# Down products of the first experts from parted rows and weights, as products of 512 and of 256 columns

## The reference

```python
w13_out = ragged_dot(x_sort, moe_w13, group_sizes)      # 256 -> 1024, by expert
gate, up = split(w13_out, [512])
hidden = silu(gate) * up
out_dispatch = ragged_dot(hidden, moe_w2, group_sizes)  # 512 -> 256: the down product
out = zeros.at[token_ids_sort].add(out_dispatch * w_sort)
```

## Time and profile before

| | us |
|---|---|
| median of 3 runs | 1511.56 |
| profiled execution | 1501.55 |
| its span | 1499.7 |
| TensorE busy (89%) | 1334.3 |
| VectorE busy (51%) | 766.2 |
| ScalarE busy (39%) | 585.5 |
| GpSimd busy (44%) | 654.1 |

### The profile page before, as it was taken

The page is one execution under the profiler, slowest core; times in us unless marked ns, Lnnn a source line. Parts: engine busy times, 40 slices in busy tenths (PEclk is TensorE's granted clock), DMA queues, the critical chain, the costliest instruction groups (busy, mean ns, idle before and its releaser), DMA issues. The chain is left out here.

```text
span 1499.7 us, 29032 instructions
## 1 busy us (share of the span) xinstructions
PE 1334.3 (89%) x7717; PEld 1055.5 (70%) x7718; DVE 766.2 (51%) x1962; ACT 585.5 (39%) x1311; POOL 654.1 (44%) x903
## 2 busy tenths in 40 slices
PE   7989999997979999999994998569999998577877
PEld 4656777775668888888883776258888885366655
DVE  4875888886822233223224886913333333154546
ACT  2555777775322222222222775533333332111110
POOL 1213656564023333333332763055555551655552
PEclk9998999998989999999996998579999999888989
DMA  2208222223721111111115885455555575333433
GB/s 92 63 29 326 91 88 84 87 79 112 281 95 50 52 52 49 49 52 52 49 39 172 260 227 178 174 182 156 158 164 164 161 141 124 103 112 106 122 115 99
DMA packets 117292, 179.69 MB, mean 120 GB/s; under 512 B 17178, under 2 KB 91947, under 8 KB 113900
## 3 DMA queue, kind: packets, MB, share of 16 engines
q1 hardware_dynamic: 80980, 100.29, 20.1%
q0 software_dynamic: 20640, 56.39, 14.2%
q10 hardware_dynamic: 15608, 22.25, 4.2%
HBM read 115.00 MB, written 59.64 MB: 116 GB/s over the span
## 5 line engine op out<-in xcount | busy, mean ns | idle before, releaser
L1228 POOL DMA_INDIRECT xg<-t_xn,token x160 | 151.3, 946 | 160.8 <-remote 61.7
L2168 POOL DMA_INDIRECT su_yg<-t_y,slot x128 | 123.2, 963 | 114.3 <-DVE su_acc L2197 44.5
L2106 PE MATMUL psum<-gu,m_xT 128*128 x640 | 153.4, 383 | 3.2 <-ACT m_xT L2037 3.2
L1465 PE MATMUL psum<-w,m_hT 128*128 x568 | 134.5, 380 | 0.8 <-ACT m_hT L1384 0.8
L1403 DVE TENSOR_TENSOR m_h<-psum,m_h 128x512 f32<-128x512 f32 x71 | 49.2, 692 | 162.7 <-ACT m_h L1378 88.9
L2106 PEld LDWEIGHTS psum<-gu,m_xT 128*128 128x128 f32 x640 | 116.5, 192 | 16.5 <-issue 3.7
L1444 PE MATMUL psum<-w,m_xT_high 128*128 x284 | 119.2, 420 | 0.0
L1444 PE MATMUL psum<-w,m_xT_low 128*128 x284 | 113.3, 399 | 0.0
L1444 PE MATMUL psum<-w_low,m_xT_high 128*128 x284 | 112.6, 396 | 0.0
L1465 PEld LDWEIGHTS psum<-w,m_hT 128*128 128x128 f32 x568 | 102.4, 190 | 12.2 <-issue 1.2
L1378 ACT ACTIVATE m_h<-psum 128x512 f32<-128x512 f32 x71 | 42.4, 597 | 151.7 <-PE psum L1444 151.7
(11 more groups left out here) (305 smaller groups left out, 3185.6 us busy)
## 6 DMA issues: line engine op xcount, KB each, us to landing
t_y<-m_y SPq DMA_DIRECT2D x80, 256.0 KB
w<-in_w SPq DMA_DIRECT2D x8, 1024.0 KB, 11.1
t_x<-at_x SPq DMA_DIRECT2D x64, 128.0 KB, 2.0
t_w_low<-at_low ACTq DMA_DIRECT2D x64, 128.0 KB, 1.7
w_low<-t_w_low SPq DMA_DIRECT2D x8, 1024.0 KB, 13.1
at_yg<-t_y SPq DMA_DIRECT2D x32, 256.0 KB, 3.5
gu<-in_gu ACTq DMA_DIRECT2D x8, 1024.0 KB, 11.8
w<-in_x SPq DMA_DIRECT2D x16, 256.0 KB, 2.7
```

What stands on the lines that cost most here:

```text
L1228: pool.indirect_dma_start(out=g.xg1[j % GB][:, k * D:(k + 1) * D], out_offset=None, in_=g.xn4, in_offset=bass.IndirectOffsetOnAxis(ap=g.to ...
L1465: last = pe.matmul(ps_y[:, 0:D], hT[:, c * P:(c + 1) * P], g.w2[:, bass.ds(ex * (MC * D) + c * D, D)], start=(c == 0), stop=(c == MC - 1))
L2106: last = pe.matmul(ps_gu[p][:, k * 2 * M1:(k + 1) * 2 * M1], xT[p][:, at:at + P], g.gu[:, bass.ds(ex[k] * (DC * 2 * M1) + c * 2 * M1, 2 * ...
L2168: pool.indirect_dma_start(out=yg[p][k][:, :], out_offset=None, in_=g.y1, in_offset=bass.IndirectOffsetOnAxis(ap=g.slot[:, at:at + 1], axis ...
```

## The change

`load_w2` is gone, and with it the loads in routing and at the stage's start. SP now loads, for every chunk, the 1024 columns of w2 of that chunk's expert into one of two buffers `raw`, at an address that it reads from `g.expert`. ScalarE rounds them into the "high" columns of `both[p]`, and VectorE subtracts to get the "low" ones. In `both` the 256 high and the 256 low columns of a contraction block stand side by side, so that one product of 512 columns with `hT_high` gives high x high in columns 0 to 255 of `ps_y` and high x low in columns 256 to 511. A product of 256 columns with `hT_low` adds low x high to the first half. VectorE makes `hT_low`, and after the down product copies the first half and adds the second. `raw`, `both`, `hT_high` and `hT_low` have two buffers each and take the space of `g.w2`.

```diff
-            load_w2(sp, g, W2_FIRST, E0, s_w2)
...
+            def load(j):
+                p = j.mod(2)
+                sp.reg_load(e[p], g.expert[0:1, bass.ds(j.n, 1)])
+                ex = sp.snap(e[p], min_val=0, max_val=E0 - 1)
+
+                wait(sp, w2_low, j.shift(-1).n)
+                sp.dma_start(raw[p][:, :], g.ins["w2"][:, bass.ds(ex * W2_COLS, W2_COLS)]).then_inc(s_raw[p], 16)
...  ScalarE, ahead of silu
+                    act.wait_ge(s_raw[p], (j.div(2).n + 1) * 16)
+
+                    wait(act, y_mm, j.shift(-1).n)
+                    act.activation(part(p, 0), whole(p), ACT.Copy).then_inc(w2_high, 1)
...
-                    wait(act, y_mm, j.n)
-                    act.activation(hT[:, :], ps_ht[:, 0:M0], ACT.Copy).then_inc(h_out, 1)
+                    wait(act, y_mm, j.shift(-1).n)
+                    act.activation(hT_high[j.mod(2)][:, :], ps_ht[:, 0:M0], ACT.Copy).then_inc(h_high, 1)
...  VectorE
+                    dve.wait_ge(w2_high, j.n + 1)
+                    dve.tensor_tensor(part(p, 1), whole(p), part(p, 0), ALU.subtract).then_inc(w2_low, 1)
...
+                    dve.wait_ge(h_high, j.n + 1)
+                    dve.tensor_tensor(hT_low[p][:, :], ps_ht[:, 0:M0], hT_high[p][:, :], ALU.subtract).then_inc(h_low, 1)
...
-                    dve.tensor_copy(y[p][:, :], ps_y[:, 0:D]).then_inc(y_out, 1)
+                    dve.tensor_copy(y[p][:, :], ps_y[:, 0:D]).then_inc(y_half, 1)
+                    dve.wait_ge(y_half, j.n + 1)
+                    dve.tensor_tensor(y[p][:, :], ps_y[:, D:2 * D], y[p][:, :], ALU.add).then_inc(y_out, 1)
...  TensorE
-                    wait(pe, h_out, j.n)
+                    wait(pe, h_low, j.n)
...
-                    pe.wait_ge(h_out, j.n + 1)
+                    pe.wait_ge(w2_low, j.n + 1)
+                    pe.wait_ge(h_low, j.n + 1)
                     wait(pe, y_out, j.n)
                     for c in range(MC):
-                        last = pe.matmul(ps_y[:, 0:D], hT[:, c * P:(c + 1) * P],
-                                         g.w2[:, bass.ds(ex * (MC * D) + c * D, D)],
+                        tile, at = slice(c * P, (c + 1) * P), 2 * c * D
+                        if c:
+                            pe.matmul(ps_y[:, 0:D], hT_low[p][:, tile], both[p][:, at:at + D], start=False, stop=False)
+                        last = pe.matmul(ps_y[:, :], hT_high[p][:, tile], both[p][:, at:at + 2 * D],
                                          start=(c == 0), stop=(c == MC - 1))
+                        if not c:
+                            pe.matmul(ps_y[:, 0:D], hT_low[p][:, tile], both[p][:, at:at + D], start=False, stop=False)
```

More of the change, by code:

```diff
@@ L1098 @@
 W2_FIRST = W2_LATE + -(-ROUTE0_SPACE // W2_COLS)
[L1101 to L1104, removed]
 class KeysValues:
@@ L1244, in route0_phase @@
         kv = KeysValues(nc, ctx, sem, g, g.bank[5:7], g.bank[7])
-        s_w2, s_beta, s_low, s_vb, r.s_pad = (sem(n) for n in ("w2", "s_beta", "s_low", "s_vb", "s_pad"))
+        s_beta, s_low, s_vb, r.s_pad = (sem(n) for n in ("s_beta", "s_low", "s_vb", "s_pad"))
         LOW = 8
@@ L1330, in moe0_phase, with rounded @@
         h = [sb(f"h{i}", [P, M0]) for i in range(2)]
[L1331 to L1335, removed]
+        raw = [g.w2[:, i * W2_COLS:(i + 1) * W2_COLS] for i in range(2)]
+        def rounded(name, at, n):
+            return nc.alloc_sbuf_tensor_at("m0_" + name, [P, n], F32R, offset=g.w2_at + at * 4)
+        both = [rounded(f"both{i}", (2 + 2 * i) * W2_COLS, 2 * W2_COLS) for i in range(2)]
+        hT_high, hT_low = ([rounded(f"hT_{name}{i}", 6 * W2_COLS + (2 * n + i) * M0, M0) for i in range(2)]
+                           for n, name in enumerate(("high", "low")))
+        passed = sem("passed_pool")
+        s_raw = [sem(f"s_raw{i}") for i in range(2)]
+        x_t, high_out, low_out, gu_mm, silu_done, h_done, h_t, h_high, h_low, w2_high, w2_low, y_mm, y_half, y_out = (
+            sem(n) for n in ("x_t", "high_out", "low_out", "gu_mm", "silu_done", "h_done", "h_t", "h_high", "h_low",
+                             "w2_high", "w2_low", "y_mm", "y_half", "y_out"))
         ps_gu, ps_x, ps_ht, ps_y = g.pair[0:2], g.bank[4], g.bank[5], g.bank[6]
@@ L1353, in _, with part, whole @@
                                             in_=y[p][:, :], in_offset=None).then_inc(y_st[p], 16)
+        def part(p, i):
+            return both[p][:, :].rearrange("p (c i n) -> p c i n", i=2, n=D)[:, :, i, :]
+        def whole(p):
+            return raw[p][:, :].rearrange("p (c n) -> p c n", n=D)
         @block.sync
         def _(sp):
-            sp.wait_ge(x_t, 1)
-            load_w2(sp, g, 0, W2_LATE, s_w2)
-            sp.wait_ge(s_w2, 16 * W2_LATE)
+            e = [sp.alloc_register(f"m0_load{i}") for i in range(2)]
+            def load(j):
[4 more added lines that the diff above has]
+                sp.dma_start(raw[p][:, :], g.ins["w2"][:, bass.ds(ex * W2_COLS, W2_COLS)]).then_inc(s_raw[p], 16)
+            steps(sp, 4, NS0 - NS0 % 2, NS0, 2, load)
+            for p in range(2):
+                sp.wait_ge(s_raw[p], (NS0 + 1 - p) // 2 * 16)
         @block.scalar
@@ L1371, in step @@
                     act.activation(xT_high[p][:, :], ps_x[:, 0:D], ACT.Copy).then_inc(high_out, 1)
+                j = s.shift(-2)
+                if j.within(NS0):
+                    p = j.mod(2)
+                    act.wait_ge(s_raw[p], (j.div(2).n + 1) * 16)
+                    wait(act, y_mm, j.shift(-1).n)
+                    act.activation(part(p, 0), whole(p), ACT.Copy).then_inc(w2_high, 1)
                 j = s.shift(-1)
@@ L2274, in program @@
             g.not_first = l0.enter_context(nc.sbuf_tensor("not_first", [P, E0 * NT], F32))
+            g.w2_at = nc.sbuf_base
             g.w2 = l0.enter_context(nc.sbuf_tensor("w2", [P, E0 * W2_COLS], F32))
```

3 lines of the change are left out of this document (removed).

## The result

| | before | after |
|---|---|---|
| median of 4 runs, us | 1511.45 (1509.12 to 1512.79) | 1491.6 (1489.61 to 1493.05) |
| ratio, 95% interval | | 0.9874 [0.9846, 0.9902] |
| profiled execution, us | 1501.55 | 1491.89 |
| its span, us | 1499.7 | 1490.0 |

The timed runs say 19.9 us faster (by the interval 15 to 23), the forecast was 21.2. The two profiled executions differ by 9.7 us only, because the one of before lies 10 us under its own timed runs. So the gain is sought in the stage, not in the span.

What follows compares the result with a forecast made beforehand. TensorE's issue was taken to bound the first experts' stage; 22.2 us saved in the steps, 1.0 lost at the start and zero at the end gave -21.2, so 1490.4 us, range 1482 to 1506.

Steps and rivals of the forecast that it cites:

- The bound: First experts' stage: set by what TensorE issues, not by a wait; busy 348.00 of 348.00 us at clock 1.00.
- The 512-column product, 0.231: Down product: each 512-column product with rounded operands takes 0.231 us, like the gate/up product in the trace.
- Rival A: Down product: TensorE needs only 0.216 us per 512-column and 0.108 per 256-column product, 29 us saved, 1483.5; chance 0.12.
- The 256-column product, 0.12: Down product: each 256-column product with a rounded weight takes 0.12 us, bounded by 0.108 and 0.216.
- The step: One chunk of 128 rows on TensorE: from 5.15 to 4.82 us, 22.2 us saved over 68 steps.
- The start of the stage, +1: Stage's start: two 512 KB loads issued beside the first gather delay it by 1 us, between 0 and 4.1.
- The end, 0: Chunks 69 to 71, without gate/up products beside them: zero change, between 1 us saved and 1.3 lost.
- The sum: Whole kernel: -22.2 + 1.0 = -21.2 us, giving 1490.4 in the timed runs.
- ScalarE and VectorE hide their new work: Beside TensorE's 4.82 us step: ScalarE needs 2.6 us and VectorE 3.9, so their added work costs nothing.
- it would bind with two more microseconds: VectorE in each step: it would bind if its two largest additions were each a microsecond longer.
- The loads: SP's queue: one 512 KB load a step, landing in 4 to 5 us with 7.3 us available, so hidden.
- rival C: Ring of weight load, copy and subtraction sets the step: 5.58 us at a landing of 8.6, 1542 us; chance 0.07.

Runs made afterwards that it cites:

- three_256: The changed kernel with each 512-column down product issued as two of 256 columns on the same stationary rows: 1416.83 us, ratio 0.9878 to the kernel before.
- late_loads2: The changed kernel with the first w2 load held back until the first x transposes are done: 1490.35 us, ratio 0.9877 to the kernel before, stage 362.01 us.
- thrice_sub: The changed kernel with VectorE's weight subtraction done three times in each step: 1575.73 us, ratio 1.0468 to the kernel before, step 6.08 us.
- release_h: The changed kernel with each w2 load released by the hT subtraction two chunks before instead of the weight subtraction: 1486.23 us, ratio 0.9869 to the kernel before.
- after_again2: The changed kernel run again unchanged, for the spread: 1489.70 us, ratio 0.9864 to the kernel before, stage 363.61 us.
- two_weights: The changed kernel with parted weights made for the first two chunks only, 69 loads, copies and subtractions left out: 1414.59 us, ratio 0.9839 to the kernel before.

## Why the prediction was right, step by step

- **The bound.** Right: TensorE's issue, 100% busy at a clock of 1.00 before and after.
- **The 512-column product, 0.231.** Right: 0.23 by starts, with fixed addresses as with moving ones. Rival A, which had TensorE fall to 0.216 and 0.108, is refuted by the same rows; the spacing that the Trainium skill gives ("TensorE: Matmul & The Clock Gate", back-to-back issue gap) doesn't hold for these rounded products here. What the difference of 0.015 to 0.018 a product consists of stays open.
- **The 256-column product, 0.12.** Right, though it was a choice between 0.108 and 0.216: 0.118 measured, and shown by three_256 not to hang on the weight load. The choice by the nearest kind (half of the gate/up product) was the good one.
- **The step.** Forecast 4.82 from 5.15, measured 4.860 from 5.175. The single step of the earlier trace rows is 0.025 under the mean of 66, so both ends shift; the difference, 0.315 for 0.326, makes 21.4 us over 68 steps for 22.2. The down product by itself has 1.50 by starts and not the 1.40 that the prediction named as a sign: its first product is followed 0.10 later than the others. The h transposes ahead of it have 0.08 less than before, so the sum of the two, which is what the step is made of, came out almost as forecast (1.85, and 0.43 + 1.40 = 1.83).
- **The start of the stage, +1.** The mis-sized term: +2.2, within the 0 to 4.1 given. late_loads2 shows that the two loads beside the gather are all of it.
- **The end, 0.** From the last x transposes on the stage is 0.6 us shorter, of which the 68th step's 0.3 is already counted above; so -0.3, within the 1 saved and 1.3 lost that were given.
- **A term that the sum didn't have.** The first to the fourth x transposes take 0.65 us less. late_loads2 has before's 10.9 us there, so about half a microsecond of the late start is caught up in these steps.
- **The sum.** The step's saving 0.8 less than forecast, the start 1.2 dearer, the end and the first steps 0.9 better: that the total is off by 1.0 us only owes something to luck, since the errors partly cancel.
- **ScalarE and VectorE hide their new work.** Right. Durations: copy 1.05 for 1.05, weight subtraction 1.23 for 1.21. That durations were added up to 3.9 us made VectorE look nearer to the bound than it is: by starts it needs 3.5 and 3.7 in turn, so the reserve is about 1.3 and not 0.9 us a step. My statement that it would bind with two more microseconds is right as far as thrice_sub goes, and the border lies at about 1.3.
- **The loads.** The lead was forecast at 7.3 and is 7.2. The landing isn't shown in the changed kernel; 5.1 us were enough for all but one. The 8.6 us of the earlier trace rows, on which rival C rested, have no like in release_h, where no load needed more than about 5.4.
- **From the stage to the time.** Stage -20.2, timed runs -19.9, forecast -21.2. That the first pair of profiles differs by 9.7 us only lies behind this stage, where the two executions of before took 697.0 and 703.3 us and those of the changed kernel 708.7 and 710.9. What varies there, and whether a part of it belongs to the change, stays open. The timed runs speak against a large part: 19.9 us saved at first and 16.5 in after_again2, with 20.2 saved in the stage.

## What to carry to other kernels

Where TensorE is the bound, price the passes over the array and don't only count them: a plain float32 product of 256 columns costs two passes of 0.216 us (0.432 a block here), three rounded products of 256 columns cost three single ones of 0.118 (0.35), and the rest is a question of whether the other engines can make the parts in the time. To ask how near an idle-looking engine is to binding, add up its operations by starts in a stretch where it is dense, not by durations, and over a whole turn of the loop, or repeat one operation until the bound's spacing changes. When an edit moves loads, look at which small transfer they will now start beside: the two loads at the stage's start cost 2 us that nothing in the steps shows, and one wait gives 1.6 of them back. And measure a stage by two marks around it, when the span of the program varies by more than the effect.

## What the runs showed of the hardware that I had not expected

- GpSimd's indirect DMA instruction stands while a VectorE operation with all operands in SBUF runs, if that one started first: 988 ns without, 1.81 and 1.92 us in the mean (by buffer) beside the 1.23 us subtraction, ending 0.86 to 0.87 us after it, with one SBUF input or two. The Trainium skill ("SBUF — State Buffer", who interferes with whom) has it that the two engines share a pair of ports as a lock: VectorE takes it in its faster modes with a single source, and with two SBUF inputs against a GpSimd instruction that reads SBUF. Both runs fit that. The same section lists `tensor_tensor` as one that was seen not to stall a DMA issued by GpSimd; the rows above disagree for this scatter.
- VectorE takes 0.69 us for 1024 float32 columns with one input from SBUF and 1.23 us with two.
- VectorE's durations overlap by up to 0.1 us, so a sum of durations of 104% of a step (5.07 of 4.86) was still possible without a wait of TensorE.
- The same program takes 1435 us on one chip and 1506 to 1511 on others, while the steps of this stage (4.86 us in two_weights and in the changed kernel) are the same on all: the difference lies outside of it. The stage ends at 781.6 us in two_weights and at 781.3 in the changed kernel; 63 of the 74 us between their spans lie in the last part of the program, from its first load of x for the last sum (`sh_x`, 154.1 and 217.3 us to the end). Why is open.
